# A graph-attention layer on one core: scores formed in one go, with one score buffer, and a re-ordered head

## The chip, the cores and the metric

The kernel runs on one core of one Trainium2 chip. The metric is the device time of one execution in microseconds (us). The kernel before takes 484.27 us, the median of 3 runs (484.2 to 484.92).

## The reference

There are 32 batches; each has `x` of 256 rows by 384 features and a 0/1 matrix `adj` of 256 by 256. Cut to what matters:

```
u = x @ x.T / sqrt(384);  p = softmax(u);  delta = p * adj
attn = delta / (sum(delta, rows) + 1e-10)
h_left, h_self, h_right = x @ W.T + b           (three weights, three biases)
ctx = (attn above the diagonal) @ h_left + diag(attn) * h_self + (attn below it) @ h_right
out = layernorm(x + relu(layernorm(ctx) * gamma + beta))
```

Everything is float32 to a tight tolerance, so the kernel splits each operand of a matmul into a high and a low part (`hi`, `lo`, type fp32r) and adds hi·hi + hi·lo + lo·hi.

## The kernel before, in words

**Tiling.** The 256 rows are T = 2 tiles of P = 128 rows, the 384 features are C = 3 chunks of 128. The batches run one after the other; each engine has its own program, written out by hand, with four batches unrolled (`every_batch`). Semaphores join the engines. The engines execute strictly in the order written.

**TensorE (PE), per batch.** Six projection groups of 9 matmuls (`project`, L437): groups 0 and 1 are the left weight for row tiles 0 and 1, groups 2 and 3 the right weight, groups 4 and 5 the self weight. Each adds onto a bias that ACT has copied into its PSUM bank beforehand (`seed_proj`, L526); there are four banks, so the seeds of groups 4 and 5 come late in the batch. Then two `attend` of 9 matmuls (L451), one per row tile.

**Scores run ahead.** Batch b works on the scores of the next ones. `cross(b+2)` (L416, after group 4) multiplies hi by lo, 6 matmuls 256 wide, into one of two score buffers. `turn_cross` (DVE, L663) transposes that 32 by 32 into `cross_turned`, and SP sends it through DRAM (`store_cross`, `load_cross` in four parts) into `cross_raw`, which is the lo·hi term. `squares(b+1)` (L425, at the start of batch b) adds hi·hi into the same score buffer, again 6 matmuls 256 wide, all four blocks of the symmetric product. `finish_scores` (DVE, L679) adds `cross_raw` and takes the row maximum, `exps` (ACT, L507) exponentiates, `deltas` (DVE, L687) multiplies by `adj`, and `turn` (DVE), `store_turned`, `load_turned` (SP, through DRAM) give the transposed `dt_raw`, which `split_delta` (ACT L540, DVE L717) splits for the attention of the next batch.

**Order around it.** In batch b, ACT does `split_delta(b)`, `split_proj(b, 0)`, `normalise(b-1)`, `split_proj(b, 1)`, `exps(b+1)`, `seed_proj(b, 4)`, `split_proj(b, 2)`, `seed_proj(b, 5)`, ... DVE does the statistics of the context of b-1, `split_delta(b)` (low part), `norm_shift(b-1)` (L748, after POOL has raised the variance to the power -1/2, L940), `split_proj(b, 0)`, `finish_scores(b+1)`, `split_proj(b, 1)`, `deltas(b+1)`, `turn(b+1)`, ..., `turn_cross(b+2)`, `residual`, `diagonal(b+1)`, `split_xt(b+3)`.

**The head.** SP loads x transposed, weights, biases (each spread to 128 partitions by its DMA, L309) and `adj` in one queue. Batch 0 has its scores with all three products at once (`first_scores`). In batch 0 SP issues, after `cross(2)`: store and load of the cross products of 2, three loads of `x` and `adj`, and only then the store of `turned(1)`:

```python
                if at.b == 0:
                    store_cross(ahead)
                    load_cross(ahead)
                    sp.dma_start(x_sb[1][:], x_rows[1]).then_inc(x_loaded[1], 16)
                if ahead.exists(BATCHES):
...
                    load(ahead.n(1), ahead.slot(UNROLL))
                if nxt.exists(BATCHES):
                    store_turned(nxt)
```

## Time and profile before

| | |
|---|---|
| median of 3 runs | 484.27 us (484.2 to 484.92) |
| profiled execution, its own time | 482.74 us |
| span in its profile | 481.0 us |
| busy: PE, DVE, ACT, POOL | 95%, 75%, 68%, 47% of the span |
| chain that ended last | PE 87%; DMA 3%; POOL, ACT, DVE, issue 2% each |
| PE by line in that chain | ps_proj L437 58%, ps_ctx L451 20%, ps_scores L425 4%, ps_scores L416 4% |

The span runs from the first to the last instruction of the profile; the execution's own time is 1.7 us longer. The chain that ended last is followed back from the last instruction; a microsecond taken from it is a microsecond of the run until another chain takes its place. Matmuls are pipelined: a row's duration overlaps the next one's, and the distance between starts tells the pace. In the chain of waits a piece of PE begins some 0.16 us after its first matmul's start in the timeline, since the piece before counts to its modelled end.

### The profile page before, as it was taken

Reading aid. Unit: us, or ns where it says so; the run is one execution under the profiler, and the core shown is the slowest. Engines: PE = TensorE matmul, PEld = TensorE weight load, DVE = VectorE, ACT = ScalarE, POOL = GpSimd, SP = SyncE. Lnnn points to the kernel's source line nnn. Section 1 sums busy time; section 2 is a strip of 40 time slices with the busy share of each in tenths; the row PEclk is TensorE's granted clock in tenths of the full one; section 3 lists DMA queues with packets and bytes.
Section 4 is the critical chain, followed back from the end, with each engine's and each line's share of the span. In section 5 each row is a group of like instructions: output and inputs, shape, how many; then the busy total and the mean of one; then the engine's idle time right before and its main releaser. Section 6 shows DMA issues by size and latency. Waiting matters only on the chain.

```text
span 481.0 us, 9617 instructions
## 1 busy us (share of the span) xinstructions
PE 455.7 (95%) x2709; PEld 453.1 (94%) x2709; DVE 360.1 (75%) x1082; ACT 325.5 (68%) x714; POOL 224.6 (47%) x297
## 2 busy tenths in 40 slices
PE   6973999999999999999999999999999999999992
PEld 6963999999999999999999999999999999999982
DVE  4645777887778888777778877778878777877756
ACT  5724666876676677667667766776777677667752
POOL 0404345455543445554444555444555544455552
PEclk9995999999999999999999999999999999999997
DMA  7654454555655555565545556564555556454221
GB/s 236 213 186 132 154 161 155 178 187 176 208 166 176 167 173 184 175 203 185 185 146 170 184 182 190 185 201 144 167 179 185 181 189 203 154 169 130 92 71 65
DMA packets 85634, 81.64 MB, mean 170 GB/s; under 512 B 7280, under 2 KB 77680, under 8 KB 85616
## 3 DMA queue, kind: packets, MB, share of 16 engines
q1 hardware_dynamic: 85616, 81.42, 53.7%
q8 instruction: 8, 0.13, 0.1%
q14 instruction: 10, 0.08, 0.1%
HBM read 52.56 MB, written 28.84 MB: 169 GB/s over the span
## 4 chain that ended last, share of the span: by engine, by line
PE 87%; DMA 3%; POOL 2%; ACT 2%; DVE 2%; issue 2%; SPq 1%; POOLq 0%; DVEq 0%; ACTq 0%
PE ps_proj L437 58%; PE ps_ctx L451 20%; PE ps_scores L425 4%; PE ps_scores L416 4%; DMA bias<-in_L_gnn_b_left 1%; DMA dt_dram<-turned 1%; POOL w_lo L926 1%; POOL rstd L940 1%; POOL shifted L948 0%; DMA dt_raw<-dt_dram 0%; ACT ps_proj L526 0%; DMA cross_dram<-cross_turned 0%; POOL scaled L944 0%; ACT normed L556 0%; ACT ps_scores L507 0%
## 5 line engine op out<-in xcount | busy, mean ns | idle before, releaser
L437 PE MATMUL ps_proj<-w_hi,xt_hi 128*128 128x384 f32 x576 | 195.0, 339 | 14.2 <-ACT ps_proj L526 14.2
L437 PE MATMUL ps_proj<-w_lo,xt_hi 128*128 128x384 f32 x576 | 194.4, 338 | 0.0
L437 PE MATMUL ps_proj<-w_hi,xt_lo 128*128 128x384 f32 x576 | 194.2, 337 | 0.0
L940 POOL TENSOR_TENSOR rstd<-var_eps,minus_half 128x4 f32<-128x4 f32 x32 | 42.5, 1329 | 190.3 <-DVE var_eps L741 187.8
L437 PEld LDWEIGHTS ps_proj<-w_hi,xt_hi 128*128 128x128 f32 x576 | 109.0, 189 | 15.4 <-ACT ps_proj L526 15.0
L437 PEld LDWEIGHTS ps_proj<-w_lo,xt_hi 128*128 128x128 f32 x576 | 108.9, 189 | 0.0
L437 PEld LDWEIGHTS ps_proj<-w_hi,xt_lo 128*128 128x128 f32 x576 | 108.8, 189 | 0.0
L530 ACT ACTIVATE proj_hi<-ps_proj 128x384 fp32r<-128x384 f32 x128 | 63.2, 496 | 53.7 <-PE ps_proj L437 53.7
L526 ACT ACTIVATE ps_proj<-bias 128x384 f32<-128x384 f32 (+1 forms) x192 | 92.6, 496 | 1.1 <-DMA bias<-in_L_gnn_b_left 1.0
L944 POOL TENSOR_TENSOR scaled<-normed,gamma_sb 128x384 f32<-128x384 f32 x62 | 63.2, 1019 | 40.2 <-ACT normed L556 40.2
L707 DVE TENSOR_TENSOR proj_lo<-ps_proj,proj_hi 128x384 fp32r<-128x384 f32 x128 | 69.3, 547 | 15.2 <-ACT proj_hi L530 14.7
L948 POOL TENSOR_TENSOR shifted<-scaled,beta_sb 128x384 f32<-128x384 f32 x62 | 69.0, 1114 | 2.4
L550 ACT ACTIVATE ps_ctx<-ps_proj,diag 128x386 f32<-128x386 f32 x64 | 35.7, 557 | 41.4 <-PE ps_proj L437 37.1
L722 DVE BATCH_NORM_STATS2 stats<-ps_ctx 128x6 f32<-128x384 f32 x64 | 36.1, 565 | 28.1 <-PE ps_ctx L451 27.8
L540 ACT ACTIVATE dt_full<-dt_raw 128x512 fp32r<-128x512 f32 x31 | 19.6, 632 | 38.6 <-DMA dt_raw<-dt_dram 34.1
L451 PE MATMUL ps_ctx<-proj_hi,dt_left 128*128 128x386 f32 x128 | 43.6, 341 | 0.7 <-issue 0.7
L451 PE MATMUL ps_ctx<-proj_hi,dt_right 128*128 128x386 f32 x128 | 43.2, 337 | 0.0
L556 ACT ACTIVATE normed<-ps_ctx,shift,rstd 128x384 f32<-128x384 f32 x62 | 38.3, 669 | 6.3 <-DVE shift L748 6.3
L566 ACT ACTIVATE out_sb<-y_sb,shift,rstd 128x384 f32<-128x384 f32 x62 | 40.2, 698 | 0.1
L451 PE MATMUL ps_ctx<-proj_hi,dt_full 128*128 128x386 f32 x128 | 38.1, 337 | 0.6 <-ACT ps_ctx L550 0.6
L755 DVE SCALAR_TENSOR_TENSOR y_sb<-shifted,x_sb 128x384 f32<-128x384 f32 x62 | 36.6, 590 | 1.9 <-POOL shifted L948 1.9
L760 DVE BATCH_NORM_STATS2 stats<-y_sb 128x6 f32<-128x384 f32 x64 | 35.9, 561 | 2.2
(87 smaller groups left out, 658.5 us busy)
## 6 DMA issues: line engine op xcount, KB each, us to landing
x_sb<-in_x SPq DMA_DIRECT2D x32, 384.0 KB, 4.4
xt_sb<-in_x_t SPq DMA_DIRECT2D x31, 384.0 KB, 3.8
out_dram<-out_sb SPq DMA_DIRECT2D x31, 384.0 KB, 2.9
adj_sb<-in_adj SPq DMA_DIRECT2D x32, 256.0 KB, 4.5
cross_dram<-cross_turned SPq DMA_DIRECT2D x31, 256.0 KB, 2.1
cross_raw<-cross_dram SPq DMA_DIRECT2D x124, 64.0 KB, 2.0
dt_dram<-turned SPq DMA_DIRECT2D x31, 256.0 KB, 2.0
dt_raw<-dt_dram SPq DMA_DIRECT2D x124, 64.0 KB, 2.1
```

The source lines that it names most:

```text
L437: mm = nc.tensor.matmul(ps_proj[bank(at, g)][:, 0:H], stationary, moving[w][:, c, :], start=False, stop=True, skip_group_check=True)
L451: mm = nc.tensor.matmul(ps_ctx[:, t, 0:HE], s, m, start=False, stop=True, skip_group_check=True)
L526: nc.scalar.activation(ps_proj[bank(at, g)][:, 0:to], bias[w][:, 0:to], ACT.Copy).then_inc(proj_seeded, 1)
L530: nc.scalar.activation(proj_hi[:, g, 0:H], ps_proj[bank(at, g)][:, 0:H], ACT.Copy).then_inc(proj_hi_ready, 1)
L556: nc.scalar.activation(normed[:, t, :], ps_ctx[:, t, 0:H], ACT.Identity, bias=shift[at.slot(2)][:, t:t + 1], scale=rstd[at.slot(2)][:, t:t ...
L566: nc.scalar.activation(out_sb[at.slot(2)][:, t, :], y_sb[at.slot(2)][:, t, :], ACT.Identity, bias=shift[nxt][:, T + t:T + t + 1], scale=rs ...
L707: nc.vector.tensor_tensor(proj_lo[:, g, 0:H], ps_proj[bank(at, g)][:, 0:H], proj_hi[:, g, 0:H].bitcast(F32), ALU.subtract).then_inc(proj_l ...
L722: nc.vector.bn_stats(stats1[:, t, :], ps_ctx[:, t, 0:H]).then_inc(stats1_ready, 1)
L755: nc.vector.scalar_tensor_tensor(y_sb[at.slot(2)][:, t, :], shifted[:, t, :], 0.0, x_sb[at.slot(UNROLL)][:, t, :], ALU.max, ALU.add).then_ ...
L940: nc.gpsimd.tensor_tensor(rstd[at.slot(2)][:], var_eps[:], minus_half[:], ALU.pow).then_inc(rstd_ready, 1)
L944: nc.gpsimd.tensor_tensor(scaled[:, t, :], normed[:, t, :], gamma_sb[:], ALU.mult).then_inc(scaled_ready[t], 1)
L948: nc.gpsimd.tensor_tensor(shifted[:, t, :], scaled[:, t, :], beta_sb[:], ALU.add).then_inc(shifted_ready[t], 1)
```

## The change

High and low parts of x transposed now lie side by side in one tile `xt_split` (high in columns 0 to 255, low behind). For each batch but the first, `cross` computes the scores in one go: for row tile 0, per chunk, one 256-wide matmul hi·hi for its own block and the off-diagonal block (`0::2` is own, cross with the other tile) and one 256-wide hi·lo; for row tile 1, one 384-wide matmul that holds its own hi·hi block and hi·lo with both tiles. The off-diagonal hi·hi block is formed once and comes back transposed with the cross products. `squares` is gone. Each row tile has a PSUM bank of 384 columns, [own | two blocks to be turned] in each group of 32 columns, and there is one score buffer instead of two, so `cross(b)` waits for `deltas(b-1)`. `finish_scores` gets one more DVE instruction: it adds the own block onto `cross_raw`, and waits for that.

```diff
-        ps_scores = [psum(f"ps_scores{i}", [P, T, L]) for i in range(2)]
+        ps_scores = psum("ps_scores", [P, T, BANK])
...
+        def blocks(t):
+            return ps_scores[:, t, 0:3 * P].rearrange("p (q k c) -> p q k c", q=Q, k=3)
+        def exponentials(t):
+            return ps_scores[:, t, 0:3 * P].rearrange("p (q e) -> p q e", q=Q)[:, :, R:3 * R]
...
             def cross(at):
                 pe.wait_ge(xt_lo_ready, at.n(1, C))
-                if at.b != 1:
-                    pe.wait_ge(delta_ready, at.n(T, -T))
-                for t in range(T):
-                    for c in range(C):
-                        mm = nc.tensor.matmul(ps_scores[at.slot(2)][:, t, :], xt(at, c, t * P, (t + 1) * P)[0], keys(xt(at, c, 0, L)[1]),
+                pe.wait_ge(delta_ready, at.n(T, 0))
+                tile = xt_split[at.slot(UNROLL)]
+                for c in range(C):
+                    nc.tensor.matmul(blocks(0)[:, :, 0::2, :], tile[:, c, 0:P], keys(tile[:, c, 0:L]),
+                    nc.tensor.matmul(blocks(0)[:, :, 1:3, :], tile[:, c, 0:P], keys(tile[:, c, L:2 * L]),
+                for c in range(C):
+                    mm = nc.tensor.matmul(blocks(1), tile[:, c, P:L], keys(tile[:, c, P:2 * L], 3),
-            def squares(at):
...
             def finish_scores(at):
+                    dve.wait_ge(cross_loaded, at.n(64, 0))
+                    own = cross_raw[:].rearrange("p a h (t r) -> p a (h t) r", t=T)[:, :, 0::T + 1, :].rearrange("p a t r -> p t a r")
+                    square = ps_scores[:, :, 0:3 * P].rearrange("p t (q k c) -> p t q k c", q=Q, k=3)[:, :, :, 0, :]
+                    nc.vector.tensor_tensor(own, own, square, ALU.add).then_inc(own_added, 1)
+                    dve.wait_ge(own_added, at.n(1, 0))
+                    nc.vector.memset(gate[:], 0.0)
```

The place of `cross` in the batch differs by batch, and `squares` is no longer at the start:

```diff
             def one(at):
-                if at.b != 0 and nxt.exists(BATCHES):
-                    squares(nxt)
                 for i, g in enumerate(order(at)):
                     project(at, g)
...
-                    if g == 4 and at.b != 0 and ahead.exists(BATCHES):
+                    if at.b == 0 and g == 4:
+                        open_context(at)
+                    if at.b == 1 and g == 0:
+                        cross(nxt)
+                    if at.b not in (0, 1) and g == (5 if at.b == 2 else 4) and ahead.exists(BATCHES):
                         cross(ahead)
-                if at.b == 0:
-                    open_context(at)
-                    squares(nxt)
-                    cross(ahead)
                 if not last(at):
                     attend(at, 0)
                 attend(at, 1)
+                if at.b == 1:
+                    cross(ahead)
```

In the head, the left and right bias are loaded as one row each from ACT's queue and spread over the partitions by a matmul with a row of ones (`spread`), then copied out by DVE (`copy_bias`); ACT makes a first one-element copy ahead of these loads; the low part of the self weight moves from POOL to DVE; ACT and DVE do `split_delta(1)` after `seed_proj(1, 4)` and after `split_proj(1, 1)`; and SP's order in batch 0 changes:

```diff
                 if at.b == 0:
+                    sp.dma_start(adj_sb[2][:], adj_rows[2]).then_inc(adj_loaded[2], 16)
+                    store_turned(nxt)
                     store_cross(ahead)
+                    load_turned(nxt)
                     load_cross(ahead)
-                    sp.dma_start(x_sb[1][:], x_rows[1]).then_inc(x_loaded[1], 16)
+                    for b in (1, 2):
+                        sp.dma_start(x_sb[b][:], x_rows[b]).then_inc(x_loaded[b], 16)
+                    return
```

How the instructions stand now. TensorE, around the end of batch 1 (the first two rows are the end of its second `attend`, the last row starts group 0 of batch 2). Before:

```order
L451 MATMUL ps_ctx<-proj_lo,dt_right 128x386
L451 MATMUL ps_ctx<-proj_hi,dt_right 128x386
L425 MATMUL ps_scores<-xt_hi 128x256 [waits cross_turned_ready]
L425 MATMUL ps_scores<-xt_hi 128x256 x5
L437 MATMUL ps_proj<-w_hi,xt_hi 128x384 [waits proj_seeded]
```

and with the change, at the same place:

```order
L473 MATMUL ps_ctx<-proj_lo,dt_right 128x386
L473 MATMUL ps_ctx<-proj_hi,dt_right 128x386
L441 MATMUL ps_scores<-xt_split 128x4x2x32 [waits delta_ready,xt_lo_ready]
L443 MATMUL ps_scores<-xt_split 128x4x64
L441 MATMUL ps_scores<-xt_split 128x4x2x32
L443 MATMUL ps_scores<-xt_split 128x4x64
L441 MATMUL ps_scores<-xt_split 128x4x2x32
L443 MATMUL ps_scores<-xt_split 128x4x64
L447 MATMUL ps_scores<-xt_split 128x384 x3
L459 MATMUL ps_proj<-w_hi,xt_split 128x384 [waits proj_seeded]
```

The squares of batch 2 are gone from here, and the whole scores of batch 3 stand behind both attends of batch 1 (from batch 3 on they stand behind group 4, where the cross products stood).

DVE, `finish_scores` in every batch but the first. Before:

```order
L707 TENSOR_TENSOR proj_lo<-ps_proj,proj_hi 128x384 [waits proj_hi_ready]
L673 MEMSET gate 128x1 [waits scores_ready,cross_loaded]
L679 ISA ps_scores,neg_max<-ps_scores,cross_raw 128x256
L679 ISA neg_max 128x1
```

and with the change:

```order
L747 TENSOR_TENSOR proj_lo<-ps_proj,proj_hi 128x384 [waits proj_hi_ready]
L711 TENSOR_TENSOR cross_raw<-cross_raw,ps_scores 128x2x4x32 [waits cross_loaded]
L713 MEMSET gate 128x1 [waits own_added]
L719 ISA ps_scores,neg_max<-ps_scores,cross_raw 128x4x64
L719 ISA neg_max 128x1
```

One instruction and one wait now stand between the low part of group 0 and the row maximum.

SP in batch 0, from the fourth transposed x on. Before:

```order
L277 DMA xt_sb<-in_x_t 128x3x256
L292 DMA cross_dram<-cross_turned 128x512 [waits cross_turned_ready]
L298 DMA cross_raw<-cross_dram 32x4x128 [waits cross_stored]
L298 DMA cross_raw<-cross_dram 32x4x128 x3
L345 DMA x_sb<-in_x 128x2x384
L273 DMA x_sb<-in_x 128x2x384
L274 DMA adj_sb<-in_adj 128x2x256
L281 DMA dt_dram<-turned 128x512 [waits turned_ready]
L287 DMA dt_raw<-dt_dram 32x4x128 [waits turned_stored]
```

and with the change:

```order
L294 DMA xt_sb<-in_x_t 128x3x256
L355 DMA adj_sb<-in_adj 128x2x256
L298 DMA dt_dram<-turned 128x512 [waits turned_ready]
L309 DMA cross_dram<-cross_turned 128x512 [waits cross_turned_ready]
L304 DMA dt_raw<-dt_dram 32x4x128 [waits turned_stored]
L304 DMA dt_raw<-dt_dram 32x4x128 x3
L315 DMA cross_raw<-cross_dram 32x4x128 [waits cross_stored]
L315 DMA cross_raw<-cross_dram 32x4x128 x3
L361 DMA x_sb<-in_x 128x2x384 x2
```

The store of `turned(1)` no longer stands behind the reloads of the cross products and behind the loads of x.

## Rows read from the trace of the kernel before

**Rows 1.** Chain of waits, one steady batch: start us, length us, what.
```profile
263.14 0.71 PE ps_scores L425 x6
263.86 7.81 PE ps_proj L437 x45
...
273.94 3.16 PE ps_ctx L451 x18
277.10 0.71 PE ps_scores L425 x6
```
**Rows 2.** Timeline of PE: group 4 of that batch; start, length, idle before.
```profile
269.94 0.34 PE L437 MATMUL ps_proj<-w_hi,xt_hi 128*128 128x384 f32 x1
```
**Rows 3.** Timeline of DVE, that batch.
```profile
264.36 0.69 DVE L717 TENSOR_TENSOR dt_full<-dt_raw,dt_full 128x512 fp32r<-128x512 f32 x1
265.94 0.16 DVE L748 SCALAR_TENSOR_TENSOR shift<-moments,rstd 128x4 f32<-128x4 f32 x1 [0.90 <-POOL rstd L940]
...
266.52 0.43 DVE L679 CUSTOM_DVE_ANT_1 ps_scores<-ps_scores,cross_raw 128x256 f32<-128x256 f32 x1
...
268.70 0.42 DVE L687 TENSOR_TENSOR delta<-ps_scores,adj_sb 128x256 f32<-128x256 f32 x1 [0.35 <-ACT ps_scores L507]
```
**Rows 4.** Timeline of ACT, that batch.
```profile
267.64 0.46 ACT L507 ACTIVATE ps_scores<-ps_scores,neg_max 128x256 f32<-128x256 f32 x1
...
268.54 0.52 ACT L526 ACTIVATE ps_proj<-bias 128x386 f32<-128x386 f32 x1
```
**Rows 5.** Timeline of POOL, that batch.
```profile
264.52 1.39 POOL L940 TENSOR_TENSOR rstd<-var_eps,minus_half 128x4 f32<-128x4 f32 x1 [5.83 <-DVE var_eps L741]
```
**Rows 6.** Timeline of DVE and POOL in another batch.
```profile
138.95 0.69 DVE L717 TENSOR_TENSOR dt_full<-dt_raw,dt_full 128x512 fp32r<-128x512 f32 x1
...
138.89 1.01 POOL L940 TENSOR_TENSOR rstd<-var_eps,minus_half 128x4 f32<-128x4 f32 x1 [5.90 <-DVE var_eps L741]
```
**Rows 7.** Waits of all engines: engine line <- waited for: us in total, times, longest.
```profile
DVE var_eps L741 <- DVE eps L733: 0.9, 6, 0.2
```
**Rows 8.** Timeline of PE, the two holes of the head.
```profile
9.77 0.45 PE L437 MATMUL ps_proj<-w_hi,xt_hi 128*128 128x384 f32 x1 [2.92 <-ACT ps_proj L526]
...
44.21 0.69 PE L437 MATMUL ps_proj<-w_hi,xt_hi 128*128 128x384 f32 x1 [10.91 <-ACT ps_proj L526]
```
**Rows 9.** Timeline of ACT, head.
```profile
7.73 0.52 ACT L502 ACTIVATE w_hi<-w_raw 128x384 fp32r<-128x384 f32 x1 [1.47 <-DMA w_raw<-in_L_gnn_W_left]
...
9.22 0.91 ACT L526 ACTIVATE ps_proj<-bias 128x384 f32<-128x384 f32 x2 [0.97 <-DMA bias<-in_L_gnn_b_left]
...
25.37 0.45 ACT L507 ACTIVATE ps_scores<-ps_scores,neg_max 128x256 f32<-128x256 f32 x1 [2.77 <-DVE neg_max L679]
...
39.78 0.63 ACT L540 ACTIVATE dt_full<-dt_raw 128x512 fp32r<-128x512 f32 x1 [11.83 <-DMA dt_raw<-dt_dram]
```
**Rows 10.** Timeline of DVE, head: batch 1's scores, and cross products of batch 3.
```profile
24.47 0.43 DVE L679 CUSTOM_DVE_ANT_1 ps_scores<-ps_scores,cross_raw 128x256 f32<-128x256 f32 x1 [3.80 <-issue]
...
48.78 0.72 DVE L663 STREAM_TRANSPOSE cross_turned<-ps_scores 128x512 f32<-128x512 f32 x1 [1.33 <-PE ps_scores L416]
...
52.26 0.57 DVE L722 BATCH_NORM_STATS2 stats<-ps_ctx 128x6 f32<-128x384 f32 x1 [0.45 <-PE ps_ctx L451]
```
**Rows 11.** Chain of waits in the head, up to the first group of batch 4.
```profile
31.25 5.01 DMA dt_dram<-turned
...
82.38 7.81 PE ps_proj L437 x45
```
**Rows 12.** Timeline of SP's queue, head: the four reloads of `dt_raw`.
```profile
36.28 1.75 SPq L287 DMA_DIRECT2D dt_raw<-dt_dram  x4
```
**Rows 13.** DMA issues of the page: count, KB each, us to landing.
```profile
cross_dram<-cross_turned SPq DMA_DIRECT2D x31, 256.0 KB, 2.1
```
**Rows 14.** Windows: stretch, length, PE, PEld, DVE, ACT, POOL busy, PEclk, DMA share, GB/s.
```profile
34.00:36.00 2.00, 0.00 (x0) 0.00 (x0) 0.00 (x0) 0.00 (x0) 0.00 (x0) 0.88 0.76 280
...
48.00:50.00 2.00, 2.00 (x11) 2.00 (x11) 1.19 (x3) 1.64 (x4) 0.00 (x0) 0.71 0.00 0
```

More of the change, by code:

```diff
@@ L352, in one @@
                     store_turned(nxt)
-                if ahead.exists(BATCHES) and at.b != 0:
+                if ahead.exists(BATCHES):
                     store_cross(ahead)
@@ L356, in one @@
                     load_turned(nxt)
-                if ahead.exists(BATCHES) and at.b != 0:
+                if ahead.exists(BATCHES):
                     load_cross(ahead)
@@ L455, in _ @@
             pe.wait_ge(zeros_ready, 1)
-            for to in (*(p[:, 0:HE] for p in ps_proj), *(ps_ctx[:, t, 0:HE] for t in range(T))):
-                mm = nc.tensor.matmul(to, zeros[:, 0:P], zeros[:], start=True, stop=True)
+            for to in ps_proj:
+                mm = nc.tensor.matmul(to[:, 0:HE], zeros[:, 0:P], zeros[:], start=True, stop=True)
             mm.then_inc(banks_opened, 1)
@@ L570, in _ @@
             first = Batch(0, 0)
+            act.wait_ge(zeros_ready, 1)
+            nc.scalar.activation(first_read[:], zeros[:, 0:1].bitcast(F32), ACT.Copy)
+            for w, vector in ((LEFT, b_left), (RIGHT, b_right)):
+                act.dma_start(bias_row[w][:], vector.partition_broadcast(1)).then_inc(bias_row_loaded[w], 16)
             split_first_xt()
@@ L795, in _ @@
             split_xt(first.plus(1))
+            for c in range(C):
+                split_weight(SELF, c)
+            turn_cross(first.plus(1))
             dve.wait_ge(ident_ready, 1)
             diagonal(first)
-            turn_cross(first.plus(1))
             split_delta(first)
@@ L803, in _ @@
             finish_scores(first.plus(1))
-            turn_cross(first.plus(2))
             deltas(first.plus(1))
             turn(first.plus(1))
+            turn_cross(first.plus(2))
             diagonal(first.plus(1))
```

109 lines of the change are left out of this document (63 added, 46 removed).

## The prediction

> **What bounds the kernel now.** I read the page first: TensorE is busy 95% of the span and makes up 87% of the chain that ended last. Then the chain of waits in time [rows 1]: from batch to batch it holds nothing but PE pieces, one squares piece of 0.71 us, five groups in 7.81, a cross piece, a sixth group, two attends in 3.16; the next squares begin 277.10 - 263.14 = 13.96 us later. PE never waits there. So a saving on PE is worth its full length, as long as what PE waits for next comes earlier than PE does. The other part is the head, where PE stands still twice [rows 8]: 2.92 us before the first projection, 10.91 us before group 4 of batch 1. Those rows and the queue behind them [rows 9, 11, 12] decide the second half of the forecast.
>
> **1. PE in a steady batch.** The pace is 0.71/6 = 0.118 us for a 256-wide matmul and 7.81/45 = 0.174 us for a 384-wide one [rows 1]. Before: 12 of 256, 1.42 us. Now 6 of 256 and 3 of 384: 0.71 + 0.52 = 1.23 us. Saved 0.19 us per batch.
>
> **2. The wait that takes its place.** Group 4 needs its seed, which ACT makes after `exps(b+1)`, which waits for DVE's row maximum. This chain starts with the end of the attends and does not move when the squares go, so PE comes to it 0.71 us earlier: at 269.94 - 0.71 = 269.23 in the batch of [rows 2]. When is the seed there? The row maximum starts 266.52 [rows 3]. In the head ACT waited for exactly this and started its exponentials 25.37 - 24.47 = 0.90 us after it [rows 9, 10]. From there to the seed's start are 268.54 - 267.64 = 0.90 us [rows 4], from a seed's start to PE 9.77 - 9.22 = 0.55 us [rows 8, 9]. Before the change the seed was ready at 268.54 + 0.55 = 269.09, with 0.85 us to spare. Now DVE also adds the own block first: the nearest instruction by shape (two inputs, one in PSUM, 128x256) takes 0.42 us [rows 3], and a wait on DVE's own result adds up to 0.2 us [rows 7]. The lower end is 0.35 (the add overlapping its neighbours), the upper 0.75 (both, and a slower read through the new pattern); I take 0.42 + 0.08 = 0.50, nearest to the row of the same shape. Then PE can start at 266.52 + 0.50 + 0.90 + 0.90 + 0.55 = 269.37: it waits 0.14 us. Between the ends this wait is 0 to 0.39 us.
>
> In some batches POOL's power takes 1.01 us in place of 1.39 us, and then the whole chain starts 0.4 us earlier and there is no wait. The rows show when: 1.39 where DVE's low part of `dt` starts before it (264.36 against 264.52) [rows 3, 5], 1.01 where it starts after (138.95 against 138.89) [rows 6]. The Trainium skill ("GPSIMD Engine Reference", Specifications) says that POOL contends with DVE instructions that have two SBUF inputs, as that one has; by that rule, too, a later `dt` helps, and the trace agrees with 0.38 us. With the change `turn_cross` and the reload of `dt` behind it come about 0.3 us later, so I expect somewhat more such batches, about one in five. The mean wait is then about 0.13 us, and a steady batch changes by -0.19 + 0.13 = -0.06 us. From batch 4 on 26 batches form scores: **-1.6 us**.
>
> **3. The head up to batch 1.** The biases no longer travel as 192 KB each in SP's queue. The first seed waits 0.97 us for one of them; but the third chunk of the left weight is landed only at 7.73 [rows 9], and ACT makes the seeds after splitting that: at about 8.15, PE starts at 8.7 in place of 9.77. The two spreading matmuls lie in the hole before that, and DVE's copies too; they cost nothing unless they last over a microsecond. Batch 0 then runs about 1.1 us ahead; `cross(1)`, now 1.23 us, stands where 0.71 stood, squares and `cross(2)` (1.42) leave its end, `open_context` waits some 0.5 us for DVE. The attends of batch 0 begin near 20.6 instead of 22.4 and end near 23.8.
>
> Then comes a wait that the one score buffer makes. Batch 1's row maximum started at 24.47, released by the reload [rows 10]; this reload comes 0.7 us earlier (23.8), the add costs 0.5, exponentials and the two `deltas` end at 27.15. `cross(2)` waits for that, while PE was done with group 0 at 25.4: it stands 1.8 us. Cross products end 28.45, are turned by 29.3, stored by 31.45 (2.1 us) [rows 13], reloaded in four parts (1.75 us to issue [rows 12], the same 2.1 to land) by 35.7. Add, maximum, `exps(2)` and the seed: 35.7 + 0.50 + 0.90 + 0.90 + 0.55, PE starts group 4 of batch 1 at about **38.6** in place of 44.21 [rows 8]. What held it before, ACT's wait for `dt_raw` until 39.78 [rows 9] behind a store of 5.01 us [rows 11], is gone: the store no longer queues behind three loads, 1 MB in all. So the hole shrinks from 10.9 to some 5.5 us; it still is there, with the trip of the cross products of batch 2 in the place of that of `dt`.
>
> **4. The head given back in batches 1 to 3.** PE's clock fell to 1.2 GHz within the old hole (a mean of 0.88 in 34 to 36 us, 0.50 until past 48) and was back in 48 to 50 [rows 14], about 5 us after PE resumed. I take the same fall, and some 3.7 us at half speed (between none and the 5 us of before, since the hole is half as long): groups 4, 5 and the attends of batch 1 end at 46.95, and `cross(3)`, now behind them, at 48.2. DVE stands at `turn_cross(3)` until then. Before, it turned these at 48.78 and came to the statistics of the second attend 3.5 us later, at 52.26 [rows 10]; now it turns at 48.4 and gets to those statistics at 52.1, while the attend itself was over at 47. So the chain of step 2 starts 5 us late in batch 2: shift near 54.6, and the reload of the cross products of 3 (turned 49.1, store 2.1, four `dt` parts ahead of it, 1.75, 2.1) lands at 55.1. Group 4 of batch 2 starts at 58.15, PE is there at 54.45: **a new wait of 3.7 us**. Then `cross(4)` behind group 5 makes the same in small: 0.7 us in batch 3. Group 0 of batch 4 starts near 80.2; it was 82.38 - 0.16 = 82.22 [rows 11]. That is -2.0 us. The wait of 3.7 us may cost clock once more: 2.92 us of standing did not lower it [rows 8], 10.91 did after some 2.4; the price is between 0 and the 2.5 us that 5 us at half speed cost before; I take 0.9, nearer to none since this hole is nearer to the 2.92. Head: **-1.1 us**.
>
> **Sum.** -1.6 - 1.1 = -2.7 us against the profiled execution's 482.74 (its span 481.0 and 1.7 around it), 480.0. That execution is 1.53 us below the median of the runs, so I forecast 484.27 - 2.7 = **481.6 us**. Runs of this kernel differ by some 0.2%, about 1 us; less cannot be told from no change. The tail (statistics, normalising and stores after the last attends) keeps its instructions.
>
> **Rivals.**
> - *No wait at the seed.* If the add costs 0.35 us or less, or most batches get the fast power, PE saves the full 0.19: 26 x -0.19 = -5, with the head 477 to 479. For it: the wait is only 0.14 us in my sum, less than the uncertainty of the add. Chance 0.25.
> - *The seed's wait outweighs the saving* (slower). Place: before group 4 in every steady batch. If add and wait cost DVE 0.62 us instead of 0.50, PE waits 0.26 us, 26 x (0.26 - 0.19) = +1.8, and the head's gain is no more than balanced; from there on it is slower. At 0.70: wait 0.34, +3.9 - 1.1 = +2.8, 487.1 us; at 0.75, 488.4. For it: PE's slack of 0.85 is surely overdrawn by the 0.71 plus the add. Against: no row of this shape takes over 0.43. Chance 0.14.
> - *Writing in pieces slows the matmuls* (slower). Row tile 0's outputs now skip 32 of every 96 columns; until now all outputs were contiguous, only the moving side was read in pieces of 32, at full pace (0.118) [rows 1]. If these six ran at half pace, +0.71 us a batch, PE has no cover: +18 us, about 500 us. The Trainium skill ("PSUM — Partial Sum Buffer", Specifications) says that any non-contiguous pattern slows matmuls significantly, which speaks against this change. No row here shows such an output; pieces of 32 elements are long, and the read side lost nothing. Chance 0.04.
> - *The head gives everything back* and more: the late `turn_cross` carries through batches 2 to 4, low clock in both. +3 us on step 4: 484 to 486. Chance 0.17.
> - *The head does better* (batch 2's wait does not arise, clock stays high): -5 us more, 476.5. Chance 0.05.
> - The forecast itself, 479.5 to 483.5: 0.35.
>
> **Chances and range.** Faster by over 0.2% (below 483.3): 0.25 + 0.05 + nearly all of 0.35 = 0.62. Within: 0.03 of the forecast and most of the fourth rival, 0.15. Slower (above 485.2): 0.23. The range leaves out the piecewise writing, the worst of the seed's wait and the best head: 476.5 to 487.5.
>
> **What would show it.** Step 1: scores 1.23 us a batch in the chain, 9 matmuls. Step 2: the view of waits names PE L459 behind ACT L550 some 25 times, 0.1 to 0.2 us each, and the batch lasts 13.90; a period of 13.77 is the first rival, over 14.0 the second, and a distance over 0.12 between L441/L443 matmuls the third. Step 3: first projection near 8.7, group 4 of batch 1 near 38.6 after a wait of 5.5. Step 4: a wait of 3 to 4 us before group 4 of batch 2, behind DVE's turning of `cross(3)`. My forecast is wrong if the period leaves 13.8 to 14.0, or if batch 4 does not start within 1.5 us of 81.

## The result, and the profile after

The changed kernel takes **484.95 us** (median of 20 runs, 483.2 to 486.72) against 483.08 us of the kernel before in the same comparison (20 runs, 481.02 to 485.2): ratio 1.0033, 95% interval 1.0019 to 1.0047. It is slower by 0.3%; a faster kernel, 481.6 us, was forecast. The profiled execution has a span of 482.8 us against 481.0.

The page of the changed kernel, TensorE's lines of parts 1, 2 and 4:

```profile
PE 462.5 (96%) x2619; PEld 452.2 (94%) x2619; DVE 368.0 (76%) x1119; ACT 326.4 (68%) x715; POOL 224.8 (47%) x294
...
PEclk9997999999999999999999999999999999999997
...
PE 84%; DVE 4%; issue 3%; POOL 3%; DMA 3%; SPq 2%; ACT 1%; POOLq 0%; DVEq 0%; ACTq 0%
```

PE has fewer scores to form and was busy for longer (before: 455.7 us). The chain of waits of the changed kernel, one steady batch (start us, length us, what), answers to [rows 1]:

```profile
264.11 8.05 PE ps_proj L459 x45
272.16 0.12 PE ps_scores L441
272.28 0.12 PE ps_scores L443
...
272.88 0.53 PE ps_scores L447 x3
273.40 1.59 PE ps_proj L459 x9
274.99 3.17 PE ps_ctx L473 x18
```

The nine scores matmuls take 273.40 - 272.16 = 1.24 us (1.23 forecast), at full pace, 0.12 us for those that write in pieces. But the 45 projections now take 8.05 us, not 7.81, and the nine behind them 1.59, not 1.56. The batch lasts 14.06 us (from group 0 of batch 5 to that of batch 30, by 25) in place of 13.96. Why is in the timeline of DVE, ACT and PE around group 4, which answers to [rows 2 to 4]:

```profile
267.48 0.41 DVE L711 TENSOR_TENSOR cross_raw<-cross_raw,ps_scores 128x256 f32<-128x256 f32 x1
267.93 0.43 DVE L719 CUSTOM_DVE_ANT_1 ps_scores<-ps_scores,cross_raw 128x256 f32<-128x256 f32 x1
```
```profile
268.83 0.45 ACT L531 ACTIVATE ps_scores<-ps_scores,neg_max 128x256 f32<-128x256 f32 x1
...
269.75 0.49 ACT L550 ACTIVATE ps_proj<-bias 128x386 f32<-128x386 f32 x1
```
```profile
269.93 0.34 PE L459 MATMUL ps_proj<-w_lo,xt_split 128*128 128x384 f32 x1
270.11 0.64 PE L459 MATMUL ps_proj<-w_hi,xt_split 128*128 128x384 f32 x2
270.58 0.34 PE L459 MATMUL ps_proj<-w_lo,xt_split 128*128 128x384 f32 x1
```
```profile
270.29 0.19 PEld L459 LDWEIGHTS ps_proj<-w_hi,xt_split 128*128 128x128 f32 x1 [0.17 <-ACT ps_proj L550]
```

The last line is the timeline of PE's weight loads (PEld) at the same place. The row "x2" holds the last matmul of group 3 and the first of group 4. Two pitches of 0.176 would be 0.35 us; from 270.11 to 270.58 it takes 0.47. PE lost 0.12 us. It lost it in two places: the first matmul of group 4 was held until its weight load at 270.29, 0.54 us after its seed's start at 269.75, and the second one followed 0.29 us behind that, in place of 0.176. The pace would put group 4's start at 270.58 - 0.17 = 270.41. Over batches 5 to 29 the loss is 0.14 us in the mean: 0.12 us, and 0.20 in every fourth batch, where POOL's power takes 1.43 to 1.44 us and not 1.39. Such a gap is too small for a row of idle time on PE; on its weight loads the view of waits counts 30 of them, three in the head (engine line <- waited for: us in total, times, longest); the kernel before had three in all:

```profile
PEld ps_proj L459 <- ACT ps_proj L550: 15.3, 30, 5.2
```

The second part is less visible: without any wait the matmuls themselves are slower. Averaged over the distances between starts in batches 5 to 29, a 384-wide projection takes **0.1761 us**, against 0.1735 before. A steady batch, put together:

| term, us per batch | forecast | measured |
|---|---|---|
| scores, 12 to 9 matmuls | -0.19 | -0.18 |
| wait for the seed of group 4 | +0.13 | +0.14 |
| slower pace, 54 projections and 18 attends | none | +0.14 |
| sum | -0.06 | +0.10 |

The head came out ahead, if not on the way that was forecast. Timeline of PE there; it answers to [rows 8]:

```profile
9.24 0.44 PE L459 MATMUL ps_proj<-w_hi,xt_split 128*128 128x384 f32 x1
...
39.83 0.69 PE L459 MATMUL ps_proj<-w_hi,xt_split 128*128 128x384 f32 x1 [4.90 <-ACT ps_proj L550]
...
59.17 0.44 PE L459 MATMUL ps_proj<-w_hi,xt_split 128*128 128x384 f32 x1 [3.30 <-ACT ps_proj L550]
```

and its stretches of low clock and of the second hole (columns as in [rows 14]):

```profile
10.00:12.00 2.00, 2.00 (x8) 2.00 (x8) 2.00 (x6) 2.00 (x7) 0.00 (x0) 0.50 1.12 348
...
40.00:42.00 2.00, 2.00 (x7) 2.00 (x8) 1.62 (x4) 1.49 (x4) 0.88 (x1) 0.50 1.06 362
...
44.00:46.00 2.00, 2.00 (x13) 2.00 (x12) 1.38 (x2) 2.00 (x5) 1.92 (x3) 1.00 0.01 2
...
56.00:58.00 2.00, 0.00 (x0) 0.00 (x0) 1.96 (x8) 1.91 (x4) 1.18 (x2) 1.00 0.87 303
```

The first of these is a stretch that the trace of the kernel before has not: PE had been busy for all of 4 to 10 us, then its clock was at 1.2 GHz (0.50 in 10 to 12 us, 0.69 in 12 to 14). The first projection came 0.53 us earlier than before, but group 2 of batch 0 started at 14.45, before at 13.41. The 18 matmuls from the first projection on took 5.21 us in place of 3.64.

Group 0 of batch 4 starts at 80.85 us, before it was 82.22: 1.37 us gained. Group 0 of batch 30 starts at 446.69, before at 445.18. So 26 batches gave back 2.88 us, and what follows 0.26 more.

### The profile page after: what moved, and what is told of

It reads as the page before. It is cut to its first block, busy times and chain, and to the rows that moved or that the text cites. A ratio compares the mean times of both kernels' runs of the same rounds, so it can differ in the third digit from the quotient of the medians.

```text
span 482.8 us, 9448 instructions
## 1 busy us (share of the span) xinstructions
PE 462.5 (96%) x2619; PEld 452.2 (94%) x2619; DVE 368.0 (76%) x1119; ACT 326.4 (68%) x715; POOL 224.8 (47%) x294
## 4 chain that ended last, share of the span: by engine, by line
PE 84%; DVE 4%; issue 3%; POOL 3%; DMA 3%; SPq 2%; ACT 1%; POOLq 0%; DVEq 0%; ACTq 0%
PE ps_proj L459 56%; PE ps_ctx L473 18%; PE ps_scores L447 3%; PE ps_scores L441 2%; PE ps_scores L443 2%; DMA dt_raw<-dt_dram 1%; SPq L304 1%; POOL scaled L992 1%; DMA cross_raw<-cross_dram 1%; POOL rstd L988 1%; PE ps_scores L405 1%; POOL shifted L996 1%; ACT ps_scores L531 1%; SPq L315 1%; DMA dt_dram<-turned 1%
## 5 line engine op out<-in xcount | busy, mean ns | idle before, releaser
L459 PE MATMUL ps_proj<-w_hi,xt_split 128*128 128x384 f32 x1152 | 314.1, 344 | 8.7 <-ACT ps_proj L550 8.7
L459 PEld LDWEIGHTS ps_proj<-w_hi,xt_split 128*128 128x128 f32 x1152 | 212.7, 190 | 15.8 <-ACT ps_proj L550 15.3
L459 PE MATMUL ps_proj<-w_lo,xt_split 128*128 128x384 f32 x576 | 195.9, 340 | 0.0
L459 PEld LDWEIGHTS ps_proj<-w_lo,xt_split 128*128 128x128 f32 x576 | 109.4, 190 | 0.0
L550 ACT ACTIVATE ps_proj<-bias 128x384 f32<-128x384 f32 (+1 forms) x192 | 91.4, 489 | 0.7 <-DVE bias L809 0.7
L996 POOL TENSOR_TENSOR shifted<-scaled,beta_sb 128x384 f32<-128x384 f32 x62 | 71.9, 1160 | 2.4
L747 DVE TENSOR_TENSOR proj_lo<-ps_proj,proj_hi 128x384 fp32r<-128x384 f32 x128 | 67.4, 545 | 2.9 <-ACT proj_hi L554 2.8
L727 DVE TENSOR_TENSOR delta<-ps_scores,adj_sb 128x256 f32<-128x256 f32 x64 | 24.2, 420 | 18.1 <-ACT ps_scores L531 18.1
L795 DVE SCALAR_TENSOR_TENSOR y_sb<-shifted,x_sb 128x384 f32<-128x384 f32 x62 | 34.4, 555 | 3.1 <-POOL shifted L996 3.1
L982 POOL TENSOR_SCALAR_AFFINE_SELECT dt_left<-dt_full 128x256 fp32r<-128x256 f32 x64 | 26.7, 417 | 19.5 <-DVE dt_full L754 19.5
```

What stands on the lines that cost most here:

```text
L459: mm = nc.tensor.matmul(ps_proj[bank(at, g)][:, 0:H], stationary, moving[w][:, c, :], start=False, stop=True, skip_group_check=True)
L550: nc.scalar.activation(ps_proj[bank(at, g)][:, 0:to], bias[w][:, 0:to], ACT.Copy).then_inc(proj_seeded, 1)
L747: nc.vector.tensor_tensor(proj_lo[:, g, 0:H], ps_proj[bank(at, g)][:, 0:H], proj_hi[:, g, 0:H].bitcast(F32), ALU.subtract).then_inc(proj_l ...
L996: nc.gpsimd.tensor_tensor(shifted[:, t, :], scaled[:, t, :], beta_sb[:], ALU.add).then_inc(shifted_ready[t], 1)
```

## The experiments

The kernel before was timed beside each group: 483.12, 483.6 and 483.59 us where there were 12 to 24 runs of it.

**Seed ahead of the exponentials** (ACT, changed kernel):

```diff
                 split_proj(at, 1)
+                seed_proj(at, 4)
                 if nxt.exists(BATCHES):
                     exps(nxt)
-                seed_proj(at, 4)
```

> The changed kernel with one step moved on ACT: the seed of group 4 comes before exps(b+1) instead of behind it. Theory A (PE waits for that seed in every steady batch, some 0.1 to 0.2 us, and in the head for 4.9 us): the waits of PE L459 for ACT L550 vanish from the steady batches, the period falls from 14.05 to 13.8-13.9 us (26 x 0.15 to 0.25 = 4 to 6 us), and the hole before group 4 of batch 1 shrinks by 2 us or more: 477 to 481 us against the changed kernel's 484.95. Theory B (the period is longer because each projection matmul is slower, 0.176 for 0.174 us): the waits are small change, the period stays at or over 14.0, and the gain is the head's alone, 1 to 2 us.

Measured: 478.6 us (9 runs), ratio to before 0.9903 (0.987 to 0.9936). The small waits are gone; the view of waits counts 5 on the weight loads in place of 30, four in the head and one in the last batch:

```profile
PEld ps_proj L459 <- ACT ps_proj L550: 6.8, 5, 2.6
```

The period is 13.92 us: the 0.14 us of waiting left, the slower pace stayed (0.1761). In the head group 4 of batch 1 starts at 37.14 (39.83), that of batch 2 at 56.08 (59.17). So some 26 x 0.14 = 3.6 us come from the steady batches and some 3 from the head, 6.4 in the medians. The seed does not need the exponentials; only its place in ACT's queue tied it to them.

**No add of the own block** (changed kernel). This kernel leaves the high-by-high products of the own blocks out of the scores:

```diff
-                    nc.vector.tensor_tensor(own, own, square, ALU.add).then_inc(own_added, 1)
-                    dve.wait_ge(own_added, at.n(1, 0))
```

> The changed kernel without DVE's add of the own block and its wait (the own blocks' high-by-high products are left out of the scores). Theory A (the add on DVE, 0.45 us with its wait, is what makes the seed late): the seed comes 0.45 us earlier, PE has no wait before group 4 in steady batches, the period falls to 13.9 (13.77 if the matmuls had the old pace). Theory B (the chain from the end of the attends over POOL's power is late by itself once the squares are gone): waits remain and the period stays above 14.0.

Measured: 481.95 us in one run, span 480.2, period 13.93, pace 0.1761, and no wait before group 4 in 23 of 25 batches. The add with its wait, 0.45 us from start to start, is what uses up PE's cover. Together with the run before it shows that the steady wait is the seed's and is worth the period's 0.14 us.

**Two shifts by 32 bytes.** One unused tile, in the changed kernel behind `first_read`, in the kernel before ahead of `gamma_sb`:

```diff
+        sb("pad", [P, 8])
```

> The changed kernel with an unused tile of 32 bytes per partition behind first_read, so that every later tile (xt_split, dt, proj) starts 32 bytes further on. Theory A (the pace of 0.1764 us per 384-wide projection matmul comes from where xt_split starts relative to other tiles; before the change these tiles lay 32 bytes off a multiple of 64): the pace goes back to 0.1736 and the period falls by 18 x 0.003 = 0.05 us, total -1 to -1.5 us. Theory B (the pace comes from the new layout of the tile itself, high and low parts side by side with 2 KB between chunks): the pace stays at 0.176 and the time within 0.2%.

> The kernel before with the same 32-byte tile ahead of gamma_sb, so that xt_hi, xt_lo, dt and proj start at a multiple of 64 bytes, as in the changed kernel. Theory A (start of the tiles decides the pace): projection matmuls go from 0.1736 to 0.176 us, the period from 13.96 to 14.1 us, total +3 to +5 us, since PE never waits there. Theory B (layout inside xt_split decides): same time within 0.2%, pace 0.1736.

Measured: the kernel before with the pad takes 487.15 us (10 runs), ratio 1.007 (1.0041 to 1.0098), at a pace of 0.1757 and a period of 14.08. With no instruction changed, the place of its tiles costs it more than the whole change did. The changed kernel with the pad takes 485.92 us (ratio 1.0052, 1.0018 to 1.0086), at 0.1767. So an SBUF tile's address sets the pace, but my first reading, that a start at an odd multiple of 32 bytes is fast, fell: with its pad the changed kernel's xt tiles start at one, and are the slowest.

**Scores of batches 3 and 4 behind group 4** (PE):

```diff
-                    if at.b not in (0, 1) and g == (5 if at.b == 2 else 4) and ahead.exists(BATCHES):
+                    if at.b != 0 and g == 4 and ahead.exists(BATCHES):
                         cross(ahead)
...
-                if at.b == 1:
-                    cross(ahead)
```

> The changed kernel with one thing moved: in batches 1 and 2 the scores of the batch after next are formed behind group 4, as in every later batch, and no longer behind the attends (batch 1) or behind group 5 (batch 2). Theory (the late turning of cross(3) is what makes the 3.3 us of waiting before group 4 of batch 2): PE's 1.24 us of scores leaves the place behind the attends, DVE turns at about 46.6 instead of 49.57, and group 4 of batch 2 starts at 55.8 to 56.4 instead of 59.17, so 2.8 to 3.4 us less: about 482 us against 484.95. Rival (the wait there comes from the trip of dt through DRAM, which starts at 42.5 in either case): group 4 of batch 2 stays within 1 us of 59.17 and the time within 1 us of 484.95. The steady period stays 14.06 under both.

Measured: 480.56 us (7 runs), ratio 0.9939 (0.9899 to 0.998). Timeline of PE, group 4 of batch 2:

```profile
56.79 0.45 PE L459 MATMUL ps_proj<-w_hi,xt_split 128*128 128x384 f32 x1 [0.77 <-ACT ps_proj L548]
```

It stands 0.77 us there in place of 3.30, and starts 2.4 us earlier, more than the 1 us that the rival allowed and 0.4 us under the theory's lower bound of 2.8; the span is 2.8 us shorter. The late turning is the cause of most of that wait. The median fell by 4.4 us, more than the trace accounts for; the interval is wide enough for either. The period stayed at 14.05.

**Both of these edits:**

> Both edits together: ACT seeds group 4 ahead of the exponentials, and the scores of batch 3 and 4 behind group 4. If the two waits are separate things the gains add: 478.6 us less the 1.9 us that batch 2 still waited with the seed first, so 476.7 to 477.5 us. If the seed moved ahead already hid what the early scores bring, it stays at 478.6. Steady period 13.92 in either case.

Measured: 475.62 us (4 runs), ratio 0.9829 (0.9778 to 0.988). They add, to within the intervals. The two profiled heads differ by more than the edit: up to group 4 of batch 1 this kernel has the instructions of the seed edit alone, and it starts that group at 35.14 us, the other at 37.14. Here the clock stayed at 2.4 GHz in 10 to 14 us, there it fell (0.50 and 0.71). 0.4 us of the difference stand at the first projection already (8.74, to 9.16); the rest is that stretch, some 1.6 us in a head.

**The four new tiles declared last** (changed kernel, the same instructions):

```diff
-        bias_row = [sb(f"bias_row{w}", [1, H]) for w in (LEFT, RIGHT)]
-        ones_row = sb("ones_row", [1, P])
-        first_read = sb("first_read", [P, 1])
         gamma_sb = sb("gamma_sb", [P, H])
...
         shifted = sb("shifted", [P, T, H])
+        bias_row = [sb(f"bias_row{w}", [1, H]) for w in (LEFT, RIGHT)]
+        ones_row = sb("ones_row", [1, P])
+        first_read = sb("first_read", [P, 1])
```

> The changed kernel, its instructions unaltered; only the four small new tiles (two bias rows, the row of ones, the first_read column) are declared last among the SBUF tiles instead of ahead of gamma, so that every tile behind the biases starts at the address that it had in the kernel before. If the place of the tiles sets the pace of the matmuls (0.1761 us against 0.1735 for a 384-wide one), the pace is 0.1735 to 0.1740, PE's work of a batch is 0.15 us shorter; the seed's wait then eats most of that (period about 14.02 instead of 14.06), since the seed's chain does not depend on the pace of the projections: total 483.5 to 485. If the pace has another cause (the run, the chip, the joined hi and lo tile), it stays 0.176.

Measured: 483.72 us (10 runs), ratio 1.000 (0.9973 to 1.0027), pace 0.1736, period 14.00. Timeline of PE in a steady batch of this kernel, around group 4:

```profile
269.39 0.34 PE L459 MATMUL ps_proj<-w_lo,xt_split 128*128 128x384 f32 x1
269.56 0.73 PE L459 MATMUL ps_proj<-w_hi,xt_split 128*128 128x384 f32 x2
270.13 0.34 PE L459 MATMUL ps_proj<-w_lo,xt_split 128*128 128x384 f32 x1
```

Two pitches take 0.57 us here, so PE now stands for 0.57 - 0.35 = 0.22 us. The pace is back, and the seed's wait takes over more than half of it: PE comes to group 4 0.09 us earlier, and the seed does not. The placement alone is worth only 14.06 - 14.00 = 0.06 us a batch as long as this wait is there.

**The kernel before once more**, for a second trace:

> The kernel before once more, unaltered, for a second trace of it: it tells whether its pace of 0.1735 us per 384-wide matmul belongs to the kernel or to the one execution that was profiled. If it belongs to the kernel: 0.1733 to 0.1737 again, period 13.96. If to the execution: 0.175 to 0.177 and a period of 14.1.

Measured: pace 0.1735, period 13.96, span 481.0 again. The pace belongs to the kernel.

**All three edits** (seed first, early scores, tiles last):

> The seed first, the early scores and the four small tiles last: with no wait before group 4 the faster pace has nothing to be eaten by. If the terms are independent: 26 batches of 13.92 - 0.15 = 13.77 us, the head as with the two edits, so 475.6 - 4.2 = 471.4 us. If a wait for ACT or DVE comes up at the faster pace instead, the period stays near 13.9 and the time near 475.

Measured: **473.16 us** (472.08 to 475.74, 4 runs), ratio 0.9745 (0.9689 to 0.98): 2.5% faster than the kernel before and the fastest one here. The period is 13.79 (13.77 expected), but the total gains 2.5 us over the two edits where 4.2 were expected, and the intervals of the two overlap. Its profiled execution was the slowest of its four: all matmuls up to 15 us ran at half pace, and the first projection started at 11.65 us, to 9.24 in the changed kernel. In its page the chain that ended last is no longer PE's, though PE waits for no seed in batches 6 to 29:

```profile
issue 28%; POOL 21%; DVE 18%; ACT 12%; DMA 10%; SPq 7%; PE 4%; DVEq 0%; POOLq 0%; ACTq 0%
```

The chain through statistics, power, scores and the two trips through DRAM now ends as late as PE's work; that a further saving on PE alone would be met by it is read from this line, not tried.

**Biases by DMA again** (changed kernel; no spreading matmuls, copies or queue of ACT):

```diff
             load_weight(LEFT)
+            load_bias(LEFT, b_left)
...
             load_weight(RIGHT)
+            load_bias(RIGHT, b_right)
...
-            spread(RIGHT)
```

> The changed kernel with the left and the right bias sent to 128 partitions by DMA again, in SP's queue where the kernel before has them (no spreading matmuls, no copies by DVE, no ACT queue); the tiles stay declared. Theory 1 (the biases were worth what the sum gave them, about 1 us of the head): the first projection starts at 9.8 in place of 9.24, the loads behind the biases are later, and the time is 0.5 to 1 us longer, 485.5 to 486. Theory 2 (the two spreads of 0.84 us on PE's path and the copy that the first seed waits for eat the gain): first projection within 0.3 us of 9.24 and the time within 0.5 us of the changed kernel's.

Measured: 487.82 us (10 runs), ratio 1.0077 (1.0046 to 1.0109). That is 2.9 us over the changed kernel by the medians and some 2.1 by the ratios (1.0077 and 1.0033, each to the kernel before in its own comparison), more than either theory gave. The first projection starts at 9.56 after 2.24 us of standing, 0.3 us late only. The loads behind the biases land up to 2.4 us later (`adj` of batch 0 at 10.14, to 7.76). PE stands 1.9 us in place of 0.5 before `cross(2)`, and group 4 of batch 1 starts at 41.47 in place of 39.83. By group 4 of batch 2 it is 2.3 us behind (61.49 to 59.17), and there its clock falls, which it did not in the changed kernel (columns as in [rows 14]):

```profile
62.00:64.00 2.00, 2.00 (x8) 2.00 (x7) 2.00 (x4) 0.64 (x2) 1.92 (x3) 0.50 0.23 92
```

So the bias change is worth 2 to 3 us, more than its 0.3 us at the first projection. By which way is not shown: the store of batch 1's cross products is only 0.25 us later (20.14, to 19.89), and 1.6 us come in behind it, where two of its four reloads land 3.3 us after their issue in place of 1.95; then comes the stretch of low clock. Whether either belongs to the biases or to this execution was not tried. The two spreads of 0.84 us, which lie on PE's path, are a price paid inside that (chain of waits of the changed kernel, head; each spread, one row of 384 float32 columns, is issued as two matmuls):

```profile
6.73 0.84 PE ps_ctx L412 x2
7.57 0.91 PE ps_scores L405 x6
8.47 0.84 PE ps_ctx L412 x2
```

**Which tiles, and what about their place.** All of these are the kernel before with unused tiles, each run once. The pads stood ahead of `xt_hi` (32, 64, 128 or 1024 bytes), behind `xt_lo` (32), ahead of everything (32), or in two places:

```diff
+        sb("pad", [P, 8])
         w_raw = [sb(f"w_raw{w}", [P, C, H]) for w in range(3)]
...
+        sb("pad2", [P, 24])
         xt_hi = [sb(f"xt_hi{i}", [P, C, L], F32R) for i in range(UNROLL)]
```

> The kernel before with an unused tile of 32 bytes declared ahead of xt_hi: the xt_hi and xt_lo tiles and all behind them move by 32 bytes; gamma, x_sb, xt_sb and adj_sb stay. If the place of the stationary operand of the projections (xt_hi, xt_lo) sets their pace: 0.1757 us per 384-wide matmul as with the pad ahead of gamma, against 0.1735. If it is the place of the tiles that DMAs write (x_sb, xt_sb, adj_sb): 0.1735.

> The same pad declared behind xt_lo: now xt_hi and xt_lo stay where they were, and only what is declared behind them (delta, dt, proj_hi, proj_lo and others) moves by 32 bytes. If the stationary operand sets the pace of the projections: 0.1735 us, and at most the attends (18 matmuls, 2.98 us from first to last start) slow down. If the tiles that ACT and DVE write do it: 0.1757.

> The kernel before with an unused tile of 64 bytes ahead of xt_hi, so that the xt_hi and xt_lo tiles move by 64 bytes. If only an odd multiple of 32 bytes makes the matmuls slow, the pace is 0.1735 us per 384-wide matmul; if the place within 128 bytes counts, it is 0.1767, as in the changed kernel with its pad, whose xt tiles lay at the same place within 128 bytes.

> The same with 128 bytes. If the place within 128 bytes is what counts: 0.1735 us, as without a pad. If the rule has a longer period or any shift is slow: 0.1757 or more.

> The kernel before with 32 bytes declared ahead of everything, so that the weights (the moving operand) and the xt tiles (the stationary one) move together and keep their distance. If the place of the stationary tiles alone sets the pace: 0.1757 us, as with the pad ahead of xt_hi. If the distance of the two operands does: 0.1735.

> The kernel before with 32 bytes ahead of the weights and 96 more ahead of xt_hi: the weights move by 32 bytes, the xt tiles by 128. If the place of the stationary tiles within 128 bytes alone sets the pace: 0.1735 us. If the moving operand's place or the distance counts: another pace, 0.1757 or more.

> The kernel before with the weights moved by 32 bytes and the xt tiles by 64, so that their distance grows by 32 bytes, as with the pad ahead of xt_hi that made the pace 0.1757 us. If the distance between the two operands sets the pace: 0.1757 again. If the weights' own place does (both kernels in which they moved by 32 bytes were fast): 0.1735.

> The kernel before with 1024 bytes ahead of xt_hi, the weights in place. If the pace depends on the distance with a period of 256, 512 or 1024 bytes: 0.1735 us. If the period is longer, or any other distance than that of the kernel before is slow: 0.176 to 0.177.

Measured, with the kernels above in their places; the shifts are those of the weight tiles and of the xt tiles against the kernel before, the four new tiles of the changed kernel being 2 x 1536 + 512 + 32 = 3616 bytes per partition (the last holds 4 bytes and is counted as 32). The pace is good to 0.0001:

| weights, xt moved by | their distance grew by | pace, us | span, us |
|---|---|---|---|
| 0, 0 (before, twice) | 0 | 0.1735 | 481.0, 481.0 |
| 0, 0 (pad behind xt_lo) | 0 | 0.1734 | 480.8 |
| 0, 0 (changed kernel, tiles last) | 0 | 0.1736 | 481.4 |
| 32, 32 | 0 | 0.1735 | 484.1 |
| 0, 1024 | 1024 = 4 x 256 | 0.1735 | 480.9 |
| 32, 128 | 96 | 0.1734 | 481.0 |
| 0, 32 (pad ahead of gamma; of xt_hi) | 32 | 0.1757, 0.1757 | 486.9, 486.1 |
| 32, 64 | 32 | 0.1757 | 487.1 |
| 0, 3616 (changed kernel) | 14 x 256 + 32 | 0.1761 | 482.8 |
| 0, 64 | 64 | 0.1767 | 487.7 |
| 0, 3648 (changed kernel, pad) | 14 x 256 + 64 | 0.1767 | 486.9 |
| 0, 128 | 128 | 0.1766 | 486.2 |

The piece of 45 projections in the chain of waits shows the same without an average. The pad behind `xt_lo`, the pad ahead of `xt_hi`, 64 bytes, and weights by 32 with xt by 64:

```profile
263.59 7.80 PE ps_proj L438 x45
```
```profile
267.16 7.92 PE ps_proj L438 x45
```
```profile
268.08 7.95 PE ps_proj L438 x45
```
```profile
268.18 7.92 PE ps_proj L439 x45
```

The tiles behind `xt_lo` do not matter to the projections. Of the two operands of the projections it is not the place of either alone: xt moved by 32 is slow with the weights in place and fast with the weights moved along. Every row agrees with a pace of the projections that is set by the **distance** between stationary tile (xt) and moving tile (weights): growth by 0, 96 and 1024 bytes fast, by 32 0.0022 to 0.0026 us slower, by 64 and 128 0.003 slower, the same again at 3616 and 3648, which are 32 and 64 above a multiple of 512. So it may repeat every 512 bytes; the last two come from the changed kernel, whose xt tiles are laid out otherwise. The theories of a place within 64 or 128 bytes fell (64 and 128 were slow), and so did that of the weights' own place (32, 64 was slow). That the distance is the cause is the reading that fits all ten placements; it is not derived from anything else, and the mechanism stays open. It does not cover everything: the six cross matmuls and the six squares, both of whose operands lie in xt tiles and keep their distance, start 0.1181 us apart in the kernel before, 0.1188 with xt moved by 32 bytes and 0.1195 with 64 or 128; and with weights at 32 and xt at 128, where the projections are fast, the scores take 0.1191 and the 18 attends 3.18 us in place of 3.16. A growth of 96 was run only with the weights moved too. Why 96 is fast, and what 160 to 224 would do, was not tried. The pads' spans differ also by their heads (the kernel with 32, 32 had its first projection at 10.40 us), so the pace, not the span, is the measure here.

## Why the prediction was wrong

- **Step 1, PE in a steady batch: right for the scores, incomplete for the rest.** 1.24 us of scores for 1.23. The step that failed is the tacit one behind it: that all other matmuls of a batch keep the pace of [rows 1]. They went from 0.1735 to 0.1761 us, 0.14 us a batch on PE, because four small tiles declared ahead of `gamma_sb` moved the xt tiles; declared last, with every instruction the same, they leave 0.1736. I read the diff's allocations as costing nothing. Undone, it gives 0.06 us a batch, 26 x 0.06 = 1.6 us, since the seed's wait takes the rest.
- **Step 2, the wait that takes its place: right mechanism, too small.** The 0.14 us measured look like the 0.13 forecast, but that is luck: the slower pace brings PE to group 4 0.09 us later. At the old pace (tiles last) PE stands 0.22 us. Of the terms, the add was 0.45 us, below my 0.50; maximum to exponentials 0.90, as taken; exponentials to seed 0.92 for 0.90; seed's start to the first matmul 0.55, as taken, in each of the 25 steady batches. What the sum left out stands behind that: after a wait the second matmul starts 0.28 us after the first and not 0.174, which is 0.11 us more for PE. The rows from which I took 0.55 had it too, in the row behind 9.77 [rows 8]:

```profile
10.06 0.34 PE L437 MATMUL ps_proj<-w_lo,xt_hi 128*128 128x384 f32 x1
```

And of the fast powers there is 1 in 25 steady batches, not one in five: the later reload of `dt` did not push DVE's low part behind the power (265.32 on DVE, 265.48 on POOL, as far apart as before; the shift then waits 0.90 us for POOL). In the working, 0.14 us in four batches of five is 0.11, not 0.13. At the old pace the term was off by 0.22 - 0.13 = 0.09 us a batch, 2.3 us: the larger part of the miss, and the rival "the seed's wait outweighs the saving" in truth (0.22 against 0.18), at a smaller add than it supposed.
- **Step 3, the head up to batch 1: right direction, not the way forecast.** First projection 9.24 (8.7 forecast), group 4 of batch 1 at 39.83 (38.6), the wait for `deltas` before `cross(2)` 0.5 us (1.8), the hole 4.9 us (5.5). "They cost nothing" was wrong for the spreads: the seed started at 8.28 (8.15), after 0.69 us of waiting for the copied bias, but PE was in the second spread until 9.24, 0.41 us later than 8.28 + 0.55. And batch 0 did not run 1.1 us ahead: at group 2 it was 1.04 us behind, by the stretch of low clock at 10 to 14 us, which the sum had not. That is why `cross(2)` had so little to wait for: with both edits, where the clock stayed up, it stands 1.9 us. The 35.7 for the reload is 35.3 by its own terms (31.45 + 1.75 + 2.1).
- **Step 4, the head given back: right.** A hole of 3.3 us before group 4 of batch 2, at 59.17 (3.7, at 58.15; the terms give 57.95), behind the late turning of batch 3's scores; moving them gave most of it back. The clock stood at 1.2 GHz from 38 to almost 44 us (0.50 and 0.51 granted) and did not fall in the second hole, so the 0.9 us I put there was none in this execution. Batch 4 began 1.37 us earlier, for 1.1 in the sum; the nearness is in part luck, since the low clock of step 3 and the 0.9 us stand against each other.
- **Rivals.** "Writing in pieces slows the matmuls" fell: 272.16, 272.28, the starts of L441 and L443 in the chain, are 0.12 us apart. By the Trainium skill ("PSUM — Partial Sum Buffer", Specifications) such a pattern should slow matmuls significantly; with 32 of every 96 columns skipped the measurement shows nothing of it. "No wait" and "the head gives everything back" fell too. Of the signs of being wrong that the prediction named, the period came (14.06, outside 13.8 to 14.0), the start of batch 4 did not (80.85).

Put together, in the profiled executions: -1.4 (head) + 2.9 (26 batches) + 0.3 (the rest) = +1.8 us, which is 482.8 - 481.0. With the tiles last the change is neutral (ratio 1.000), still not the 0.6% forecast: 2.3 us of that difference are step 2, the rest is within the intervals.

## What to carry to other kernels

When a saving on the bounding engine leaves only a few tenths of slack, look for what the next releaser has ahead of it in its own queue: here a bias copy stood behind exponentials that it did not need, and moving one line was worth 6 us. A declaration is part of a change: moving tiles in SBUF changed the pace of untouched matmuls by 1.3 to 1.8%, so compare the distance between matmul starts before and after, and put new small tiles behind the hot ones. And price a wait on PE up to the matmul from which the pace is back, not to the first one: here 0.11 us lay between, and 26 batches multiplied it.

## What was not expected of the hardware

- The pace of a 384-wide fp32r matmul (0.1735, 0.1757 or 0.1767 us) goes with the distance in SBUF between its stationary and moving tiles, in ten placements; 256-wide scores with both operands from the xt tiles stayed within 0.118 to 0.12 us, but moved too.
- Distance isn't the whole story: in the second trace of the kernel before, batches 1 and 2 ran at 0.1765 and 0.1763 before all later ones at 0.1735 (in the first trace, groups 0 to 3 of batch 1 alone, at 0.1769), and with 128 bytes of pad batch 0 ran at 0.1738 and all later ones at 0.1766. What sets the pace in the head stays open.
- After PE has waited for a seed, the second matmul starts 0.28 us after the first at 2.4 GHz, in place of 0.174, in the steady batches of the changed kernel and at 9.77 us of the kernel before; at 1.2 GHz it is 0.49 in place of 0.32 (44.21 us there).
- POOL's power on 128x4 takes 1.39 us or more when DVE's low part of `dt` (L717, which reads two SBUF tiles) has started before it, and 1.01 to 1.03 when that starts after it or not near it. How long the two overlap does not decide: 0.52 us of overlap in the slow ones, 0.69 in two fast ones of the kernel before (138.95 against 138.89 is one, [rows 6]).
- Heads differ between executions by more than this change moved. A stretch at 1.2 GHz that begins between 9 and 11.5 us stands in 6 of the 9 traces of the changed kernel and its variants and in 5 of the 11 of the kernel before and its padded ones; in two more of the changed kernel's variants PE was at half pace from the start to 15 us. It makes the first 18 projections take 4.9 to 5.3 us in place of 3.6 to 4.1. What brings it stays open: PE had stood for 1.8 to 3.6 us before its first projection in six of these eleven traces and not at all in five, and for 0.7 to 3.1 us in six of those that kept the clock. How often it comes in the runs that have no trace is not known, so the medians can't be freed of it.
- The granted clock reads 1.00 from the start of every trace here, but the matmuls begin at half pace in all of them: in the kernel before four of 386 columns take 1.65 us (0.32 apart), and the scores come to full pace at about 4.8 us. In the profiled execution of all three edits that moment is 15 us, six 256-wide scores take 1.65 us there, where the changed kernel's take 0.97, and the column still reads 1.00. So ahead of its first fall the column tells nothing; the distance between starts does.

```profile
1.40 1.65 PE L457 MATMUL ps_proj<-zeros 128*128 128x386 f32 x4 [1.40 <-DVE zeros L772]
```
- A plain float32 matmul of one row by 384 columns takes 0.84 us in the changed kernel's head, in two passes.
